# Block-diagonal keys and values by SyncE transfers, and the value product in two halves

## The reference, cut to what matters

```python
qkv = jnp.einsum('sbh,oh->sbo', ln1, qkv_weight).reshape(S, B, NKV, (q_per_kv + 2) * HD)
scores = jnp.einsum('bgqsd,bgtd->bgqst', qb, kb) * scale
scores = jnp.where(causal, scores, jnp.finfo(scores.dtype).min)
attn = jax.nn.softmax(scores, axis=-1)
ao = jnp.einsum('bgqst,bgtd->bgqsd', attn, vb)          # then reshaped to (S, B, H)
h1 = hidden_states + jnp.einsum('sbh,oh->sbo', ao, proj_weight)
x = _layer_norm(h1, ln2_weight, ln2_bias)               # router, top 2 of 8 experts, weighted sum
return h1 + moe_out
```

## Time and profile before

| | |
|---|---|
| runs before, us | 1200.04, 1201.92 (median), 1207.69 |
| profiled execution | its page gives a span of 1207.2 us from first to last instruction; of the time around the span it gives nothing, and the nearest run is the slowest, 1207.69 |
| PE busy | 1128.8 us, 94% |
| PE weight loads (PEld) | 1016.7 us, 84% |
| VectorE busy | 910.1 us, 75% |
| ScalarE busy | 824.1 us, 68% |
| POOL busy | 587.6 us, 49% |
| mean granted TensorE clock | 0.968 of full speed |
| mask product (L1774), whole run | 64 instructions, 42.0 us |
| output copy (L1609), whole run | 128 instructions, 46.6 us |
| value product (L1385), whole run | 512 records, 68.0 us |

### The profile page before, as it was taken

The page is one execution under the profiler, slowest core; times in us unless marked ns, Lnnn a source line. Parts: engine busy times, 40 slices in busy tenths (PEclk is TensorE's granted clock), DMA queues, the critical chain, the costliest instruction groups (busy, mean ns, idle before and its releaser), DMA issues. The chain is left out here.

```text
span 1207.2 us, 25130 instructions
## 1 busy us (share of the span) xinstructions
PE 1128.8 (94%) x8180; PEld 1016.7 (84%) x8180; DVE 910.1 (75%) x2230; ACT 824.1 (68%) x1869; POOL 587.6 (49%) x564
## 2 busy tenths in 40 slices
PE   7899999999999899998998998899999999999994
PEld 4699999999998688877787776789998899889884
DVE  5677777677775579888898886897877777777872
ACT  2466666766666588887886778557677766776671
POOL 0012212122222144787888786678865454555446
PEclk9899999999999899998999998989999999999998
DMA  9533435343331022344444355578887686777654
GB/s 300 125 106 122 121 114 161 109 140 118 99 104 54 18 80 80 116 133 134 129 133 135 111 170 180 161 174 218 196 198 180 167 194 179 188 182 175 166 141 63
DMA packets 117838, 171.25 MB, mean 142 GB/s; under 512 B 13584, under 2 KB 88752, under 8 KB 117680
## 3 DMA queue, kind: packets, MB, share of 16 engines
q1 hardware_dynamic: 91120, 135.43, 36.7%
q0 software_dynamic: 26592, 34.24, 14.9%
HBM read 103.76 MB, written 67.69 MB: 142 GB/s over the span
## 5 line engine op out<-in xcount | busy, mean ns | idle before, releaser
L1311 POOL DMA_INDIRECT out_rows<-y,row x142 | 235.4, 1658 | 173.1 <-DVE y L1931 129.6
L1862 DVE TENSOR_TENSOR hl<-h,hh 128x512 fp32r<-128x512 f32 (+1 forms) x156 | 99.7, 642 | 83.7 <-ACT h L1530 73.0
L178 PE MATMUL gh<-w2h,hh 128*128 128x256 f32 x568 | 159.7, 281 | 1.1 <-issue 1.1
L180 PE MATMUL gh<-w2h,hl 128*128 128x256 f32 x568 | 159.8, 281 | 0.0
L179 PE MATMUL gh<-w2l,hh 128*128 128x256 f32 x568 | 159.6, 281 | 0.0
L1529 ACT ACTIVATE hh<-gw 128x512 fp32r<-128x512 f32 (+1 forms) x78 | 44.1, 565 | 126.9 <-issue 125.2
L1289 POOL DMA_INDIRECT slot_rows<-kept,slot x104 | 112.0, 1077 | 29.6 <-issue 28.4
L178 PEld LDWEIGHTS gh<-w2h,hh 128*128 128x128 f32 x568 | 107.8, 190 | 2.3 <-issue 1.2
L844 POOL TENSOR_SCALAR spread<-mv 128x2 f32<-128x2 f32 x32 | 7.0, 218 | 210.1 <-DVE mv L992 209.8
L179 PEld LDWEIGHTS gh<-w2l,hh 128*128 128x128 f32 x568 | 107.9, 190 | 1.1
L180 PEld LDWEIGHTS gh<-w2h,hl 128*128 128x128 f32 x568 | 107.8, 190 | 0.0
(11 more groups left out here) (338 smaller groups left out, 3945.9 us busy)
## 6 DMA issues: line engine op xcount, KB each, us to landing
w1e<-in_moe_w SPq DMA_DIRECT2D x39, 512.0 KB
w2e<-in_moe_w SPq DMA_DIRECT2D x39, 512.0 KB
xr<-slot_rows SPq DMA_DIRECT2D x32, 532.0 KB
x_rows<-x SPq DMA_DIRECT2D x64, 256.0 KB, 2.5
xg<-x_rows SPq DMA_DIRECT2D x62, 256.0 KB
xT<-in_xT SPq DMA_DIRECT2D x32, 256.0 KB, 2.8
x<-in_x SPq DMA_DIRECT2D x32, 256.0 KB, 3.7
out_rows<-res SPq DMA_DIRECT2D x64, 128.0 KB
```

What stands on the lines that cost most here:

```text
L178: nc.tensor.matmul(out, at_a(ah), at_b(bh), start=first, stop=False, skip_group_check=True)
L180: return nc.tensor.matmul(out, at_a(al), at_b(bh), start=False, stop=last, skip_group_check=True)
L1311: g.indirect_dma_start(out=out, out_offset=bass.IndirectOffsetOnAxis(ap=row[m % NR][:, t:t + 1], axis=0), in_=y[m % 2][:, t, :], in_offset ...
L1862: v.tensor_tensor(hl[m % 2][:, f, 0:n], h[:, f, 0:n], hh[m % 2][:, f, 0:n].bitcast(F32), ALU.subtract).then_inc(hl_did, 1)
```

## The change

Two tiles are added to the program: `keys0` (keys of both places, block-diagonal, 4 heads apart) and `values` (the same for the values); in the opening they serve as the memory of `xT` and `stack`. A second tile `keys1` is there during Positions, so keys have two buffers and values one. The tiles are zeroed once by POOL memsets, two at the end of the opening and one at the start of Positions. After that SyncE copies each head's 16 partitions from `pr.kv` to their place: 4 transfers of keys (16 partitions x 2 places x 512 bytes) and 8 of values (16 partitions x 4 positions x 128 bytes) a step. Those of step 0 are issued at the end of the opening; for step j+3 they are issued ahead of SyncE's store j. SyncE's hardware loop becomes straight code, and its load now goes ahead of its store in all steps. The mask product is gone from VectorE. PE puts both mask products ahead of the scores, waits for the keys' and the values' transfers, and does the value product in two halves of 64 moving columns each, into partitions 0 to 63 and 64 to 127. ScalarE then copies the attention's output with one instruction a place, and takes the queries of place 1 ahead of the copies `pwT`. The last x12 rows go to `keys0`.

```diff
+        self.keys0 = sb("keys0", [P, U2, NKV, TG, S])
+        self.values = sb("values", [P, U2, TG, NKV, S])
...
+    def fetch_keys(self, sp, keys, k):
+        groups = slice(U2 * k, U2 * (k + 1))
+        for g in range(NKV):
+            rows = slice(g * HD, (g + 1) * HD)
+            sp.dma_start(keys[rows, :, g].rearrange("p u t s -> p u (t s)"),
+                         self.kv[rows, groups].rearrange("p g t s -> p g (t s)")).then_inc(self.keys_in[k % 2], 16)
+
+    def fetch_values(self, sp, k):
+        for g in range(NKV):
+            rows = slice((NKV + g) * HD, (NKV + g + 1) * HD)
+            for u in range(U2):
+                sp.dma_start(self.values[rows, u, :, g], self.kv[rows, U2 * k + u]).then_inc(self.values_in, 16)
...
@@ opening, SyncE @@
             pipeline(step, 0, I1 + 2)
+            sp.wait_ge(pr.cleared, 2)
+            for u in places:
+                after(sp, dve_did["kv"], I1 - 1, u)
+            pr.fetch_keys(sp, pr.keys0, 0)
+            pr.fetch_values(sp, 0)
...
@@ opening, GpSimd @@
-            pipeline(step, -2, I1 + 2)
+            pipeline(step, -2, I1 + 1)
+            for u in places:
+                after(pool, dve_did["u"], I1 - 1, u)
+            g.memset(pr.keys0[:], 0.0).then_inc(pr.cleared, 1)
+            for u in places:
+                after(pool, pe_did["layer"], I1 - 1, u)
+            g.memset(pr.values[:], 0.0).then_inc(pr.cleared, 1)
+            pipeline(step, I1 + 1, I1 + 2)
...
@@ Positions, SyncE @@
             def load_last(u):
-                after(sp, pe_did["vT"], LAST, u)
+                after(sp, pe_did["score"], LAST - 1, U2 - 1)
...
-            with sp.Fori(0, EARLY_STORES) as j:
-                for u in places:
-                    store(j, u)
-                    load(j + 1, u)
-            sp.wait_ge(pr.planned, 1)
-            sp.wait_ge(pr.scattered[0], 16 * K * EARLY_GROUPS)
+            def blocks(k):
+                if k == 1:
+                    sp.wait_ge(pr.cleared, 3)
+                else:
+                    after(sp, pe_did["score"], k - 2, U2 - 1)
+                pr.fetch_keys(sp, keys[k % 2], k)
+                after(sp, pe_did["vT"], k - 1, U2 - 1)
+                pr.fetch_values(sp, k)
+
             def step(j):
+                if j + 3 < I2:
+                    blocks(j + 3)
+                if j == EARLY_STORES:
+                    sp.wait_ge(pr.planned, 1)
+                    sp.wait_ge(pr.scattered[0], 16 * K * EARLY_GROUPS)
                 for u in places:
                     after(sp, pool_did["res"], j, u)
                     if j + 1 < LAST:
                         load(j + 1, u)
                     store(j, u)
+            for k in (1, 2):
+                blocks(k)
+            for j in range(EARLY_STORES):
+                step(j)
             step(EARLY_STORES)
             pr.fetch_x(sp, 0)
             step(EARLY_STORES + 1)
...
@@ Positions, GpSimd @@
+            g.memset(keys1[:], 0.0).then_inc(pr.cleared, 1)
...
@@ Positions, PE @@
+                    pe.wait_ge(pr.keys_in[k % 2], 16 * NKV * (k // 2 + 1))
+                    for u in places:
                         after(pe, act_did["q"], k, u)
-                        after(pe, dve_did["kv"], k, u)
                         for t in range(TG):
                             ins = t_.matmul(ps_s[u][:, t * P:(t + 1) * P], qg[u][:, t].rearrange("p j s -> p (j s)"),
-                                            kvd[u][0:KV1, t].rearrange("p g s -> p (g s)"),
+                                            keys[k % 2][0:KV1, u, :, t, :],
...
+                    pe.wait_ge(pr.values_in, 16 * U2 * NKV * (k + 1))
+                    for u in places:
+                        values(k, u)
...
-                            ins = t_.matmul(ps_w[u][0:KV1, t * P:(t + 1) * P], vb[(k - 1) % 2][u][:, t, :],
-                                            pwT[u][:, t].rearrange("p j s -> p (j s)"), start=True, stop=True)
+                            for jp in range(2):
+                                ins = t_.matmul(ps_w[u][jp * KV1:(jp + 1) * KV1, t * KV1:(t + 1) * KV1],
+                                                vb[(k - 1) % 2][u][:, t, :], pwT[u][:, t, jp::2, :],
+                                                start=True, stop=True)
...
@@ Positions, ScalarE @@
                 exponentials(1)
+                if has(k + 1):
+                    heads(k + 1, 1)
                 if has(k - 1):
...
-                if has(k + 1):
-                    heads(k + 1, 1)
...
-                        pairs = ps_w[u][0:KV1].rearrange("p (t h j s) -> p j h t s", t=TG, h=2, j=2)
-                        for jp in range(2):
-                            ins = a.copy(aoT[u][jp * KV1:(jp + 1) * KV1], pairs[:, jp])
-                        ins.then_inc(act_did["ao"], 1)
+                        a.copy(aoT[u][:], ps_w[u][:, 0:TG * KV1].rearrange("p (t h s) -> p h t s", t=TG, h=2)
+                               ).then_inc(act_did["ao"], 1)
...
@@ Positions, VectorE @@
-                v.tensor_tensor(kvd[u][:], pr.kv[:, group(k, u)].unsqueeze(2).broadcast_to([P, TG, NKV, S]),
-                                pr.cst[:, C_HEAD:C_HEAD + NKV].unsqueeze(1).unsqueeze(3)
-                                .broadcast_to([P, TG, NKV, S]), ALU.mult).then_inc(dve_did["kv"], 1)
```

More of the change, by code:

```diff
@@ L382, in __init__ @@
         self.blank = sb("blank", [P, ROW])
+        self.keys_in = [self.sem(f"keys_in{n}") for n in range(2)]
+        self.values_in, self.cleared = self.sem("values_in"), self.sem("cleared")
         self.scattered = [self.sem(f"scattered{k}") for k in range(3)]
@@ L431, in opening @@
         x = bufs("x", [P, TC, D])
-        xT = bufs("xT", [P, DC, T])
-        stack = bufs("stack", [STACK, 2, D])
+        xT = [pr.keys0[:, u].rearrange("p g t s -> p (g t s)").rearrange("p (c n) -> p c n", c=DC) for u in places]
+        stack = [pr.values[0:STACK, u].rearrange("p t g s -> p (t g s)").rearrange("p (k n) -> p k n", k=2) for u in places]
         uT = parts("uT", [P, DC, T])
@@ L1056, in rows_and_experts @@
         qg = brief("qg", [KV1, TG, JQ, S])
-        kvd = brief("kvd", [P, TG, NKV, S])
-        last12 = [a[:].rearrange("p t g s -> p (t g s)").rearrange("p (k n) -> p k n", k=2) for a in kvd]
+        keys1 = passing.enter_context(nc.sbuf_tensor("keys1", [P, U2, NKV, TG, S], F32))
+        keys = [pr.keys0, keys1]
+        last12 = [pr.keys0[:, u].rearrange("p g t s -> p (g t s)").rearrange("p (k n) -> p k n", k=2) for u in range(U2)]
         rows12 = lambda j, u: last12[u] if j == LAST else x12[u][:]
@@ L1081, in rows_and_experts @@
         pe_did = {n: sem(f"gpe_{n}_") for n in "score vT wT av h nT logit".split()}
[L1082 removed]
+        dve_did = {n: sem(f"gdve_{n}_") for n in "max sub sum rden h1 st mv shift".split()}
         act_did = {n: sem(f"gact_{n}_") for n in "q exp wT v ao nT logit nrm".split()}
@@ L1323, in _, with values @@
             t_ = nc.tensor
+            def values(k, u):
+                after(pe, act_did["v"], k - 1, u)
+                for t in range(TG):
+                    ins = t_.transpose(ps_v[u][:, t * KV1:(t + 1) * KV1], pr.values[KV1:P, u, t].rearrange("p g s -> p (g s)"),
+                                       pr.cst[KV1:P, C_ID + KV1:C_ID + P])
+                ins.then_inc(pe_did["vT"], 1)
             def step(k, has):
@@ L1791, in step @@
                                         ALU.subtract).then_inc(dve_did["sub"], 1)
-                        next(route, None)
-                if has(k + 1):
-                    for u in places:
-                        heads(k + 1, u)
                         next(route, None)
```

29 lines of the change are left out of this document (6 added, 23 removed).

## The result

Four runs of the changed kernel took 1219.09 to 1237.04 us, median 1227.93; the kernel before took 1204.81 in the same comparison. The ratio is 1.0193, with a 95% interval of 1.0150 to 1.0236: slower, by some 23 us. I had forecast 1194 with a range up to 1218. All ratios compare executions in the fast state, so single long ones, 2621 us of no_transfers and 1804 us of before_nomask, are not in them. The profiled execution of the changed kernel has a span of 1224.9 us (before: 1207.2), so the profiles account for 17.7 of the 23 us.

The account below looks back on a forecast made before the run. PE was taken to bound steps 3 to 9, POOL the scatter half. Steps 3 to 9 +0.2, scatter half -12.2, start +2.7, end +1.5 sum to -7.8 us: 1194 us against the median 1201.92, range 1184 to 1218.

Parts of the forecast that it names:

- the price of an issue: SyncE in Positions: 0.46 us a transfer, 16 issues a step in 7.4 us, under 9.6, so SyncE keeps up.
- The rival named 0.60: SyncE or its transfers become the bound, from 0.60 us an issue: 1215 us, 1239 at 0.70; chance 0.15.
- POOL's floor: Scatter half of Positions, steps 9 to 31: POOL bounds at 9.63 us a step, 22 steps 211.9 us.
- 9.3 us for a quiet step with the new order: PE's steps without routing: ScalarE's new order delays pwT, so quiet steps go from 8.95 to 9.3 us.
- halves side by side: PE's value product: both column halves run at once, taking 0.95 us where it took 1.89.
- The rival with halves one after the other: PE's value product keeps 1.89 us, next step at P+9.88, over POOL's 9.63: 1204 us; chance 0.27.
- the one with unhidden loads: PE's half-width weight loads don't hide: value product 3.8 us, step 11.8, 1253 us; chance 0.05.
- 8.2 us of waits: Scatter half: without the mask product most of POOL's 10.2 us of waiting for VectorE's moments goes, 2 us kept.
- 5.7 of stretched scatters: POOL's scatters beside a mask product take 1.40 us, not 0.98; without it the 5.7 us go whole.
- the forecast start: Start of Positions: 12 SyncE issues after VectorE's last key columns make it 1.3 us later, at about 400.5.
- Transposes 1: PE's value transposes of step 1, start of Positions: values issued only after transposes 0 make them some 1.4 us late.
- the tail: End of Positions: keys and values 31 issued behind the first experts' rows come 0 to 4 us late, +1.5 us.

Follow-up runs that it names:

- no_transfers: Changed kernel without the transfers of keys and values, and PE's waits for them, from step 3 on: 1221.07 us, ratio to before 1.0106.
- before_nomask: Kernel before without VectorE's mask product from step 3 on, nothing put in its place: 1198.52 us, ratio to before 0.9926.
- order_whole: Changed kernel with ScalarE's queries of place 1 behind the normalized rows and the value product whole, transfers kept: 1226.61 us, ratio to before 1.0191.
- order_no_whole: Changed kernel with ScalarE's old order, the value product whole and no key or value transfers from step 3 on: 1199.58 us, ratio to before 0.9969.
- twelve: Changed kernel with ScalarE's old order, PE's masks and scores place by place, values position-innermost (12 SyncE issues a step): 1205.79 us, ratio to before 0.9997.
- before_order: Kernel before with only ScalarE's new order, queries of place 1 ahead of the copies pwT: 1213.24 us, ratio to before 1.0044.
- order_back: Changed kernel with ScalarE's queries of place 1 behind the normalized rows again: 1224.69 us, ratio to before 1.0138.
- before_halves: Kernel before with only the value product in halves and one output copy a place: 1201.68 us, ratio to before 0.9945.
- order_no: Changed kernel with ScalarE's old order and no key or value transfers from step 3 on: 1202.89 us, ratio to before 0.9964.
- twelve_whole: The kernel twelve with the value product whole: 1202.60 us, ratio to before 0.9977.
- whole_back: Changed kernel with the value product whole again and two output copies a place: 1224.53 us, ratio to before 1.0131.
- order_values4: Changed kernel with ScalarE's old order and keys and values stored position-innermost, 12 SyncE issues a step: 1254.91 us, ratio to before 1.0383.
- fill: Changed kernel with four extra mask products on PE ahead of the value product, read by nothing: 1224.70 us, ratio to before 1.0151.

## Why the prediction was wrong

**What failed first: the price of an issue.** I took 0.46 us for the new transfers, "since these have fewer rows than either", so 7.4 us for 16 issues, and concluded that "SyncE keeps up". They cost 0.63 at the least, a step's round is 9.8 us without a held issue and 10.3 to 10.5 on the mean, above POOL's 9.63, and SyncE is a bound. The rival named 0.60 as the point from which this decides, and it came true as a mechanism; its number, 1215, was still 13 us too low. The pair order_whole and order_no_whole prices it at 27 us where the order is the old one. Landings were no part of it: twelve moves the same bytes and PE doesn't wait for them. The upper bound of the earlier trace rows, 0.70, was the nearer one. The number of rows was no guide: the x12 load has 128 rows of 2 KB and was issued in 0.33 to 0.58, a transfer of keys has 32 rows of 512 bytes and one of values 64 rows of 128 bytes, and both are usually issued in 0.59. What makes the difference between the DRAM transfers and these, no run shows.

**What failed second: that halves and the new order stay under POOL's floor.** I had 9.3 us for a quiet step with the new order and measured 9.48; the floor of 9.63 stands, as the table under before_nomask shows. At full clock the loop does lie under it, by 0.15 us. In before_order, where the clock stays at 0.97, the order costs 5 us in all, 3.1 in steps 3 to 9 and 0.2 in POOL's 22 steps, close to what I had put, 0.35 a quiet step and 2 us. But the sum had no term for the clock, and with halves it falls: in no_transfers PE's steps from 10 on take 9.48 to 9.86 us at a mean clock of 0.96 or more and 11.1 or more at one under 0.8. There the order costs 17 us (1.0106 against 0.9964), and 17.1 us in POOL's 22 steps (235.8 against 218.7). That the order costs this much beside halves is shown by this pair; that it does so through the clock is argued from the lengths of the steps, since no run has the new order with the whole product and no transfers.

**Why the total is not the sum.** Order alone (no_transfers) gives 1.0106, SyncE alone (order_back, order_whole) 1.0138 and 1.0191, both together (the changed kernel) 1.0193. Each holds the step at 10.3 to 10.7 us. That is why four edits, each touching one thing, came back with 1.0106 to 1.0151.

**The value product: right in size, wrong in worth.** I took 0.95 us for halves side by side and forecast pairs within about 1 us; 1.17 was measured, against 1.96 whole. The rival with halves one after the other fell, as did the one with unhidden loads. The Trainium skill's "TensorEngine Tiling (Array Packing)", section "Tiling Modes", says that different tiles can load weights and multiply in parallel; the trace agrees, with 32 records of half width in 1.17 us. What I had no term for is the clock: in five pairs of kernels that differ in this part (before_halves and before, order_no and order_no_whole, twelve and twelve_whole, changed and whole_back, order_back and order_whole) it is 0.89, 0.92, 0.91, 0.86, 0.89 with halves and 0.97, 0.99, 0.97, 0.96, 0.96 whole. Alone the part is worth 0.55%, 7 us. In the other pairs the intervals overlap. In the half with scatters a shorter product can't show at all where POOL is the bound.

**The mask product: right in mechanism, a little too high.** I counted 8.2 us of waits and 5.7 of stretched scatters, 13.9 together; before_nomask gives 9, interval 5 to 13, and a profiled stage 11.4 us shorter (28 steps at 9.68 and not 10.09), 10.6 of it in POOL's 22 steps. The scatters went back to 1002 ns in the mean, also in the changed kernel, so it was the mask product that stretched them. The prediction cited the Trainium skill's page "SBUF — State Buffer", section "Who interferes with whom", for the rule that a `tensor_tensor` should not hold up the writing of descriptors. The same section also says that a VectorE instruction with two SBUF inputs does contend with a GpSimd instruction that reads SBUF. The mask product has two such inputs, so the stretch need not contradict the page; which part of a scatter was held up, no run shows. In the changed kernel the gain is swallowed, and POOL waits for the moments for longer than before: 29.3 us from 490 to 720, against the 15.9 of the earlier trace rows.

**Start and end: the forecast start was hit by luck.** The stage starts at 400.59 us (forecast about 400.5), but from VectorE's last key columns to that point it is 9.4 us:

```profile
389.71 1.50 DVE L1009 TENSOR_SCALAR kept<-pd,bqkv 128x256 f32<-128x256 f32 x2 [0.26 <-PE pd L180]
...
400.59 1.01 PE L1386 MATMUL gs<-causalb,identb 128*128 128x512 bf16 x2 [5.48 <-PEq L441]
```

Before, it is 4.3 (394.90 to 399.22). I had put 1.3 more, and it is 5.1, in all kernels with these 12 issues 5.0 to 5.1; with 8 issues (twelve, twelve_whole, order_values4) it is 2.4 to 2.5. It did not show because in this profile the opening came to its end 3.7 us earlier; the other kernels with the same opening start the stage at 400.9 to 407.0. Up to step 3 the loss against the last key columns is 3.7 us, where the sum had 2.7. Transposes 1 waited 1.75 us for the values (forecast 1.4); the tail is 2.1 longer (forecast 1.5).

By the prediction's own stretches: steps 3 to 9 took 72.0 us on PE (427.19 to 499.20), where I had 65.1 and the kernel before 65.0. POOL's 22 steps from 9 to 31 took 240.2 (496.90 to 737.09), where I had 215.9 and the kernel before 228.1. Two sums of the prediction are a little off, without weight for the result: what is left of 16.2 us after 10.2 is 6.0 and not 5.7, and SyncE at 0.70 gives 1237 and not 1239.

What stays open: what in PE's work makes the clock fall. That halves bring it down and extra full-width products (fill) bring it up is shown; by what rule the chip decides is not.

## What to carry to other kernels

Before work moves to a DMA queue, count the issues of a step and price them by transfers of the same kind in the trace; take the high price where it has none, and compare the product with the step. Where undoing one part of a change gives little, undo two together before the theory falls: two bounds of equal height hide each other, and only the pair shows it. And a path that lies under a floor by 0.15 us is not hidden: a lower clock in some steps lifts it over. Where a floor is a true one, as POOL's 9.63 us here, look for gains there first; a shorter product elsewhere can't show.

## What the hardware showed that I had not expected

- SyncE is held 0.59 us by the issue of an SBUF to SBUF transfer of 16 partitions (0.63 from one to the next), whether it moves 8 KB or 16 KB, against 0.33 to 0.58 for the x12 load of 256 KB in the same queue. The size moved is no guide to the cost.
- Products in column halves lower the granted clock. In before_halves the clock falls to a mean of 0.83 over steps in which PE is busy 99% of the time, so a shorter product made some steps longer (10.0 us against 8.95).
- The stride of an operand that PE reads costs time on both sides: 1.9 times for the moving operand (3.22 against 1.71 us for 13 records), part of it the clock of 0.87, and 1.5 times for the stationary one (212 against 138 ns a load). The Trainium skill's page "SBUF — State Buffer", section "Door 1: The DMA port swizzle", says that SBUF has lines of 16 bytes and that each access to another line pays; at a stride of four 4-byte words every access does so, and the trace agrees.
